# One batch per scan group in a Mamba and mixture-of-experts block: experts beside half of the scan, decay in PSUM

## The chip, the cores and the metric

The kernel runs on one core of a Trainium2 chip, in one launch. The metric is the device time in microseconds. A core has five engines with a queue of instructions each: TensorE (PE in the profile, its weight loads PEld), VectorE (DVE), ScalarE (ACT), GpSimd (POOL) and SyncE (SP, here for DMAs only). They wait for each other by semaphores. The order on each engine is the order in which the program's text issues the instructions; nothing reorders it.

## The reference, cut to what matters

The input x is 4 batches of 128 channels and 256 tokens. The first half of the block is a Mamba layer over four chunks of 32 channels, the second a mixture of 16 experts. All arithmetic is float32.

```python
# first half, for each batch and each of 4 chunks (32 channels -> 64 inner)
xn = layer_norm(x); xi, z = split(xn_chunk @ in_proj)
xc = silu(causal_conv4(xi) + conv_b)
dt_raw, B, C = split(xc @ x_proj)                 # ranks 2, 16, 16
dt = softplus(dt_raw @ dt_proj + dt_b)
for t in range(256):                              # state h: 64 x 16
    h = exp(dt_t * A) * h + (dt_t * xc_t) * B_t
    y_t = sum over the 16 states of h * C_t
y = (y + xc * D) * silu(z); ym = y @ out_proj + skip * xn_chunk
x = x + layer_norm(ym) @ proj + proj_b
# second half, for each token of 128 channels
t = layer_norm(x); logits = t @ router            # 16 experts
w0, w1 = softmax(top 2 of logits)
out = x + sum over e of w_e * ((silu(t @ gate_e) * (t @ up_e)) @ down_e)   # 128 -> 256 -> 128
```

## The kernel before, in words

**Groups and steps.** A tile has 128 partitions and 512 columns. In the scan two chunks of 64 inner channels fill the partitions. A scan group (`gr`) is one pair of chunks for a half of the batches (`hb`, two batches of 256 tokens side by side), so there are four groups; the two groups of half 0 come first. A group has 16 steps, one per state number s; step k = 16 gr + s. In a step:

- PE spreads row s of B over the partitions (`spread_b`), and later row s of C (`spread_c`), each one matmul from 64 rows (`bank<-BC,sel`);
- ACT makes the decay `exp(A_s dt)` in SBUF (`decay`, L447), two steps ahead in a ring of three, and copies B from its PSUM bank to SBUF for POOL (`copy_b`, L441) in the steps whose input POOL makes;
- POOL (`scan_input`, L288) or, for odd steps below 50, DVE (`input_on_dve`, L638) multiplies dt x by B to the input u;
- DVE runs two scans of 256 columns, one per batch (`scan`, L650), and multiplies the states by C (`weigh`, L661);
- PE adds the result into a PSUM bank by an identity matmul (`sum_state`); from step 48 on POOL adds it in SBUF instead (`add_state`, L295).

Behind the last step of a half, a **back chain** of 13 items (`back(hb, i)` on PE, ACT and DVE) does the output projection, two layer norms, the projection, the router, top 2 and the gates, for 512 tokens at once.

**Experts.** A slot is one expert and one half f of its 256 hidden channels, for the 512 tokens of a half: 64 slots. Gate and up products are three passes in a reduced format (high and rest parts of weights and tokens, `product`, L938, L939, L808), each of 512 columns. ACT takes the tanh of the gate (L512), DVE gates (`gate`, L748) and multiplies by the up product (`hidden`, L762); the tokens come scaled by the expert's weight (`scale_tokens` on DVE, L744, `round_scaled` on ACT, L499, `split_scaled` on POOL, L301). `down` adds into one bank, in float32 for the first half, in three reduced passes for the second.

**Stages.** Front (load, norm, projections, convolution, softplus of group 0); steps 0 to 49 alone, with the softplus polynomials of later groups, one of six DVE operations per step, and the back chain of half 0 in steps 33 to 47; then 14 expert slots of half 0 with one step each (`beside`); then the back chain of half 1 in the slots behind them (`back_item`; its PE items 3, 7 and 11 are put behind the next slot's gate product, `LATE`), then the experts of half 1. `keep_warm` issues small matmuls whose result nobody reads; steps 0 to 7 have two each, ahead of `spread_b`.

**Banks.** Before, two PSUM banks for B and two for C, alternating, to step 49; gate and up products have two banks each.

## Time and profile before

| | |
|---|---|
| runs | 388.32, 388.85, 393.81 us; median 388.85 |
| profiled execution | 391.65 us, span 389.8 us |
| PE | 338.6 us busy, 87% |
| DVE | 334.0 us, 86% |
| POOL | 199.6 us, 51% |
| ACT | 196.5 us, 50% |
| mean granted TensorE clock | 0.881 |

The span reaches from the first to the last instruction; 1.85 us of the profiled time lie around it. A line such as `L650 DVE TENSOR_TENSOR_SCAN ring<-ring 128x256` names the source line, engine, operation and tiles (`ring` holds u, the copy of B, the states, the weighed states and the decays; `bank` is PSUM). In a timeline the first number is the start and the second the length, up to the last write; the next instruction of the engine can start a little before that, so a cost in a full queue is taken from start to start. `x2` behind a row is two instructions merged. A float32 matmul stands as two records. What follows in brackets is the idle time of the engine ahead of the row and who ended it. The clock column gives the granted TensorE clock: 1.00 is 2.4 GHz, 0.50 is 1.2 GHz, and a value between them a stretch with both.

### The profile page before, as it was taken

What the parts mean: (1) busy time and instruction counts of PE and PEld (TensorE: products, weight loads), DVE (VectorE), ACT (ScalarE), POOL (GpSimd) and SP (SyncE); (2) the same over time, 40 slices, a digit from 0 to 9 for tenths busy, and PEclk for the clock granted to TensorE, in tenths of its full rate; (3) what the DMA queues carried; (4) which work ended last, traced back from release to release, by engine and by line L of the source; (5) the groups of instructions that cost most, each with busy time, mean ns of one, the idle gap of its engine ahead of it and who ended that gap; (6) DMA issues with size and microseconds to landing.
All of it is one profiled execution on the core that took longest, in us unless ns stands there. A gap on an engine that the chain in (4) does not pass through costs nothing. (4 is left out here: it accounts for less than half of the span.)

```text
span 389.8 us, 3634 instructions
## 1 busy us (share of the span) xinstructions
PE 338.6 (87%) x986; PEld 173.1 (44%) x986; DVE 334.0 (86%) x518; ACT 196.5 (50%) x303; POOL 199.6 (51%) x167
## 2 busy tenths in 40 slices
PE   8793769997979879877878778799998999999996
PEld 5420434432223222232334334345565667777774
DVE  2699999779999999999999999996769686667774
ACT  3974622243434544464745554236783366666661
POOL 4447661224232331321477777745562277888882
PEclk9987565557586999996989998899999999999999
DMA  6592000000000000000000000000000000000000
GB/s 201 168 280 90 2 1 1 0 0 1 0 3 0 0 0 0 1 2 0 0 0 2 0 0 2 0 0 1 2 1 0 1 29 0 1 2 0 0 3 27
DMA packets 6644, 7.95 MB, mean 20 GB/s; under 512 B 352, under 2 KB 5472, under 8 KB 6624
## 3 DMA queue, kind: packets, MB, share of 16 engines
q1 hardware_dynamic: 6480, 7.34, 6.3%
q10 hardware_dynamic: 144, 0.38, 0.3%
q8 instruction: 8, 0.13, 0.2%
q14 instruction: 12, 0.10, 0.1%
HBM read 7.20 MB, written 0.52 MB: 20 GB/s over the span
## 5 line engine op out<-in xcount | busy, mean ns | idle before, releaser
L650 DVE TENSOR_TENSOR_SCAN ring<-ring 128x256 f32<-128x256 f32 x128 | 107.6, 880 | 0.0
L288 POOL TENSOR_TENSOR ring<-dtx,ring 128x512 f32<-128x512 f32 x39 | 56.3, 1445 | 97.0 <-ACT ring L441 63.8
L808 PE MATMUL bank<-BC,sel 64*128 64x512 f32 x128 | 55.7, 592 | 33.9 <-DVE ring L661 23.0
L447 ACT ACTIVATE ring<-dt,cst,A 128x512 f32<-128x512 f32 x64 | 51.3, 809 | 52.7 <-DVE ring L650 52.2
L512 ACT ACTIVATE dt<-bank,cst 128x512 f32<-128x512 f32 x64 | 44.0, 687 | 58.1 <-PE bank L808 58.1
L808 PE MATMUL bank<-ring,ident 128*128 128x512 f32 x96 | 70.0, 818 | 0.3 <-DVE y L670 0.2
L808 PEld LDWEIGHTS bank<-BC,sel 64*128 64x128 f32 x128 | 20.9, 217 | 104.3 <-DVE ring L661 59.5
L748 DVE SCALAR_TENSOR_TENSOR dt<-dt,bank 128x512 f32<-128x512 f32 x64 | 43.8, 684 | 26.5 <-ACT dt L512 26.5
L301 POOL TENSOR_TENSOR xs_lo<-xc,xs_hi 128x512 fp32r<-128x512 f32 x32 | 43.7, 1364 | 28.0 <-ACT xs_hi L499 28.0
L661 DVE TENSOR_TENSOR ring<-ring,bank 128x512 f32<-128x512 f32 x63 | 41.9, 664 | 3.9 <-PE bank L808 3.8
L441 ACT ACTIVATE ring<-bank 128x512 f32<-128x512 f32 x39 | 22.9, 586 | 28.2 <-PE bank L808 28.2
L938 PE MATMUL bank<-tn_hi,Wg_hi 128*128 128x512 f32 x64 | 32.0, 500 | 0.0
L938 PE MATMUL bank<-xs_hi,Wu_hi 128*128 128x512 f32 x64 | 28.0, 437 | 0.0
L295 POOL TENSOR_TENSOR y<-y,ring 128x512 f32<-128x512 f32 x15 | 19.3, 1285 | 14.9 <-DVE ring L661 14.9
L499 ACT ACTIVATE xs_hi<-xc 128x512 fp32r<-128x512 f32 x32 | 20.0, 625 | 13.1 <-DVE xc L744 13.1
L808 PE MATMUL bank<-xs_hi,Wu_lo 128*128 128x512 f32 x64 | 25.9, 404 | 0.0
L939 PE MATMUL bank<-xs_lo,Wu_hi 128*128 128x512 f32 x64 | 25.8, 403 | 0.0
L808 PE MATMUL bank<-tn_hi,Wg_lo 128*128 128x512 f32 x64 | 25.4, 397 | 0.0
L939 PE MATMUL bank<-tn_lo,Wg_hi 128*128 128x512 f32 x64 | 25.4, 397 | 0.0
L808 PEld LDWEIGHTS bank<-ring,ident 128*128 128x128 f32 x96 | 18.1, 236 | 15.9 <-issue 14.2
L333 POOL TENSOR_TENSOR hid_lo<-y,hid_hi 128x512 fp32r<-128x512 f32 x16 | 20.7, 1294 | 8.7 <-ACT hid_hi L506 8.7
L762 DVE TENSOR_TENSOR zs<-dt,bank 128x512 f32<-128x512 f32 x32 | 21.8, 682 | 2.8 <-DVE dt L748 0.4
(134 smaller groups left out, 561.0 us busy)
## 6 DMA issues: line engine op xcount, KB each, us to landing
ring<-gate_w SPq DMA_DIRECT2D x4, 256.0 KB, 5.0
ring<-up_w SPq DMA_DIRECT2D x4, 256.0 KB, 5.3
X<-x SPq DMA_DIRECT2D x2, 256.0 KB, 4.3
sq<-gate_w SPq DMA_DIRECT2D x2, 256.0 KB, 2.7
xm<-gate_w SPq DMA_DIRECT2D x2, 256.0 KB, 3.6
sq<-up_w SPq DMA_DIRECT2D x2, 256.0 KB, 3.5
xm<-up_w SPq DMA_DIRECT2D x2, 256.0 KB, 2.7
out<-X SPq DMA_DIRECT2D x2, 256.0 KB, 2.1
```

The costliest lines, as they stand in the source:

```text
L288: g.tensor_tensor(u[:, k % 3], dtx[:, k // NS, :], Bs[:, copies(k) % 3], ALU.mult)\
L301: g.tensor_tensor(xs_lo[:, k % 2, :], xs, xs_hi[:, k % 2, :].bitcast(F32), ALU.subtract)\
L441: a.activation(Bs[:, copies(k) % 3], bank[b_bank(k)][:], ACT.Copy).then_inc(S["Bs_r"], 1)
L447: a.activation(dA[:, k % 3], dt[:, k // NS, :], ACT.Exp, scale=A[:, s:s + 1], bias=zero)\
L512: a.activation(th[:, f, :], bank[GATE[f]][:], ACT.Tanh, scale=0.5, bias=zero).then_inc(S["th_r"], 1)
L650: v.tensor_tensor_scan(h[:, k % 3, t], dA[:, k % 3, t], u[:, k % 3, t], 0.0, ALU.mult, ALU.add).then_inc(S["scan_r"], 1)
L661: v.tensor_tensor(dst, h[:, k % 3], bank[c_bank(k)][:], ALU.mult).then_inc(S["hc_r"], 1)
L748: v.scalar_tensor_tensor(th[:, f, :], th[:, f, :], 1.0, bank[GATE[f]][:], ALU.add, ALU.mult)\
L762: v.tensor_tensor(hid[k % 2][:, f, :], th[:, f, :], bank[UP[f]][:], ALU.mult).then_inc(S["hid_r"], 1)
L808: return t.matmul(o, w, r, start=start, stop=stop).then_inc(S[name], 1)
L938: t.matmul(bank[b][:], w_hi, hi, start=first, stop=False)
L939: t.matmul(bank[b][:], w_hi, lo, start=False, stop=False)
```

## The change

- **Groups.** A group is one batch with all four chunks: the two pairs lie side by side in the 512 columns. The back chain of batch b needs group b alone and has 256 columns. It runs in turns (`group_turn`): turn o of batch b at step 16 (b+1) + o. Batch 0's runs in steps 16 to 31, those of batches 1 and 2 beside the experts and steps 32 to 63, batch 3's beside items 32 to 47.
- **Experts.** An item is one expert for one batch, both hidden halves side by side: 64 items. Its products are twelve passes of 256 columns. Items 0 to 31 have one step each (steps 32 to 63). While they do, gate and up have one bank each (`gate_bank`, `up_bank`). Down is in reduced passes for the last 16 items only. The tokens of two items are scaled by one DVE operation; the gates' spread reads 128 rows.
- **Scan.** The decay goes to a PSUM bank: two banks in steps 0 to 31, one afterwards (`da_bank`), and `decay` waits for the scan that last read it. The first column of each pair is kept at zero, so one scan of 512 columns serves both pairs. All inputs u are POOL's. C has one bank. States are summed by PE up to step 31, by POOL from 32 on.
- **Norms.** A matmul with `M` (identity less mean) gives centred values straight into PSUM; output projection, skip, norm gain and bias are folded into prepared weights.
- **Softplus.** The logarithm's polynomial is written as two quadratics, each a Square on ACT into PSUM and one DVE operation, where DVE had six; the input's positive part and magnitude come from DVE, the final sum from POOL.
- **Loads.** Each weight chunk has its own staging buffer; eight of sixteen are rounded and split during steps 2 to 23.

The three item loops at the end of the diff are ACT's, DVE's and PE's, in this order.

```diff
-POOL0 = 3 * NS
-LEAD_END = POOL0 + 2
-SCAN_SLOTS = 14
-LATE = (3, 7, 11)
+FIRST = 2 * NS
+ITEMS = BATCH * E
+BESIDE = STEPS - FIRST
+SPLIT0 = 3 * E
...
+        def da_bank(k):
+            return k % 2 if k < FIRST else 0
+        def gate_bank(n):
+            return 1 if n < BESIDE else (1, 0)[n % 2]
+        def up_bank(n):
+            return 5 if n < BESIDE else (5, 2)[n % 2]
...
+        def step_at(slot):
+            return FIRST + slot
+        def group_turn(k, first=1):
+            b, o = divmod(k, NS)
+            return (b - 1, o) if b - 1 in range(BATCH) else (None, None)
...
             def decay(k):
-                if k >= 3:
-                    act.wait_ge(S["scan_r"], 2 * (k - 2))
+                if k % NS == 0:
+                    act.wait_ge(S["dt_r"], k // NS + 1)
+                if before(da_bank, k):
+                    act.wait_ge(S["scan_r"], before(da_bank, k))
                 s = k % NS
-                a.activation(dA[:, k % 3], dt[:, k // NS, :], ACT.Exp, scale=A[:, s:s + 1], bias=zero)\
-                    .then_inc(S["dA_r"], 1)
+                rows = [v.rearrange("p (q t) -> p q t", t=T)[:, :, 1:T] for v in (bank[da_bank(k)][:], dt[:, k // NS, :])]
+                a.activation(rows[0], rows[1], ACT.Exp, scale=A[:, s:s + 1], bias=zero).then_inc(S["dA_r"], 1)
...
+            for n in range(ITEMS):
+                k = step_at(n)
+                gate_tanh(n)
+                if k + 1 < STEPS:
+                    decay(k + 1)
                 if k + 3 < STEPS:
                     copy_b(k + 3)
+                back(*group_turn(k), True)
+                if n % 2 == 0 and n // 2 + 1 < ITEMS // 2:
+                    round_scaled(n // 2 + 1)
...
             def scan(k):
-                for b in range(2):
-                    t = slice(b * T, (b + 1) * T)
-                    v.tensor_tensor_scan(h[:, k % 3, t], dA[:, k % 3, t], u[:, k % 3, t], 0.0,
-                                         ALU.mult, ALU.add).then_inc(S["scan_r"], 1)
+                v.tensor_tensor_scan(h[:, k % 3], bank[da_bank(k)][:], u[:, k % 3], 0.0, ALU.mult, ALU.add)\
+                    .then_inc(S["scan_r"], 1)
...
+            def factor_1(b):
...
+                v.scalar_tensor_tensor(part, bank[R][:], LOG1P_SCALE * QUAD1[1], dt[:, b, :], ALU.add, ALU.mult)\
+                    .then_inc(S["t1_r"], 1)
...
+            for n in range(ITEMS):
+                k = step_at(n)
+                if n % 2 == 0 and n // 2 + 1 < ITEMS // 2:
+                    scale_tokens(n // 2 + 1)
+                gate(n)
+                if k < STEPS:
+                    scan(k)
+                hidden(n)
+                if FIRST < k <= STEPS:
+                    weigh(k - 1)
+                back(*group_turn(k))
...
+            for n in range(ITEMS):
+                k = step_at(n)
+                if n % 2 == 0 and n // 2 + 1 < ITEMS // 2:
+                    spread_gate(n // 2 + 1)
+                gate(n)
+                if FIRST < k <= STEPS:
+                    spread_c(k - 1)
+                if k + 3 < STEPS:
+                    spread_b(k + 3)
+                up(n)
+                for j in downs(n):
+                    down(j)
+                back(*group_turn(k))
```

On ACT beside the experts, before, with the semaphores waited for (L512 tanh, L447 decay, L441 copy of B, L499 rounding of the scaled tokens):

```order
L512 ACTIVATE dt<-bank,cst 128x512 [waits hid_r,g_r]
L447 ACTIVATE ring<-dt,cst,A 128x512 [waits scan_r]
L441 ACTIVATE ring<-bank 128x512 [waits u_r,pB]
L499 ACTIVATE xs_hi<-xc 128x512 [waits up_r,xs_r]
L512 ACTIVATE dt<-bank,cst 128x512 [waits hid_r,g_r]
```

The same place in the change, up to turn 3 of a back chain (L512 tanh, L463 decay, L454 copy of B, L506 rounding, L478 a Square of the back chain):

```order
L506 ACTIVATE xs_hi<-xc 128x512 [waits up_r,xs_r]
L512 ACTIVATE dt<-bank,cst 128x512 [waits hid_r,g_r]
L463 ACTIVATE bank<-dt,cst,A 128x2x255 [waits scan_r]
L454 ACTIVATE ring<-bank 128x512 [waits u_r,pB]
L478 ACTIVATE sq<-bank,cst 128x256 [waits op_r]
L512 ACTIVATE dt<-bank,cst 128x512 [waits hid_r,g_r]
```

The order of the kinds is the same; the decay between two tanh operations is now that of the next step and waits for the scan of this one, and the back chain stands between them while steps still run.

On PE, the variance matmul of the second layer norm in half 1, before (L938, L939 and L808 with `Wg` the gate product, with `Wu` the up product):

```order
L938 MATMUL bank<-tn_hi,Wg_hi 128x512 [waits m_r]
L939 MATMUL bank<-tn_lo,Wg_hi 128x512
L808 MATMUL bank<-tn_hi,Wg_lo 128x512
L808 MATMUL bank<-sq,mean_w 128x512 [waits sq_r]
L938 MATMUL bank<-xs_hi,Wu_hi 128x512 [waits hid_r]
```

The same matmul in the change, turn 7 of batch 1 (L990 the down product of an earlier item, L931 the next gate product):

```order
L990 MATMUL bank<-y,Wd 128x256 [waits hid_r]
L990 MATMUL bank<-y,Wd 128x256
L794 MATMUL bank<-sq,mean_w 128x256 [waits tsq_r]
L794 MATMUL bank<-CE,sel_e 128x256 [waits xs_r,cel_r]
L794 MATMUL bank<-CE,sel_e 128x256
L931 MATMUL bank<-tn_hi,Wg_hi 128x256 [waits m_r]
```

It stood behind the next slot's gate product and now stands ahead of it.

## Rows read from the trace of the kernel before

**Rows 1.** Busy time by stage: start:end, length, then busy us (x instructions) of PE, PEld, DVE, ACT, POOL.
```profile
48.50:84.30 35.80, 32.52 (x63) 14.17 (x63) 30.80 (x46) 9.46 (x14) 12.19 (x9) 0.54 0.00 0
84.30:123.00 38.70, 34.28 (x60) 10.81 (x60) 38.66 (x61) 15.67 (x23) 12.08 (x9) 0.68 0.00 1
123.00:190.20 67.20, 54.56 (x134) 18.77 (x132) 66.78 (x127) 33.22 (x51) 17.84 (x14) 0.95 0.00 0
190.20:256.70 66.50, 52.94 (x149) 26.75 (x148) 65.62 (x81) 31.18 (x48) 49.47 (x35) 0.92 0.00 0
256.70:312.20 55.50, 54.20 (x184) 31.82 (x184) 42.57 (x84) 32.02 (x49) 25.18 (x20) 1.00 0.00 1
312.20:383.50 71.30, 71.30 (x286) 52.03 (x284) 50.49 (x77) 44.11 (x75) 56.17 (x45) 1.00 0.01 5
```

**Rows 2.** Timeline of DVE, one step at the high clock: start, length, engine, line, operation.
```profile
130.04 1.26 DVE L650 TENSOR_TENSOR_SCAN ring<-ring 128x256 f32<-128x256 f32 x2
131.23 0.65 DVE L661 TENSOR_TENSOR ring<-ring,bank 128x512 f32<-128x512 f32 x1
131.81 0.67 DVE L638 TENSOR_TENSOR ring<-dtx,bank 128x512 f32<-128x512 f32 x1
```

**Rows 3.** Timeline of DVE, one slot with a step beside it.
```profile
220.38 0.68 DVE L748 SCALAR_TENSOR_TENSOR dt<-dt,bank 128x512 f32<-128x512 f32 x1
220.98 2.42 DVE L650 TENSOR_TENSOR_SCAN ring<-ring 128x256 f32<-128x256 f32 x2
223.32 0.66 DVE L762 TENSOR_TENSOR zs<-dt,bank 128x512 f32<-128x512 f32 x1
```

**Rows 4.** Timeline of POOL in the same stretch.
```profile
224.66 1.29 POOL L295 TENSOR_TENSOR y<-y,ring 128x512 f32<-128x512 f32 x1 [0.19 <-DVE ring L661]
```

**Rows 5.** Timeline of PE at the low clock, in and after the padded steps.
```profile
73.14 1.22 PE L819 MATMUL bank<-mean_w 128*128 128x128 f32 x4
...
81.62 0.79 PE L808 MATMUL bank<-BC,sel 64*128 64x512 f32 x2
82.34 2.07 PE L808 MATMUL bank<-ring,ident 128*128 128x512 f32 x2
```

**Rows 6.** Timeline of PE at the high clock, the same two steps.
```profile
86.46 0.51 PE L808 MATMUL bank<-BC,sel 64*128 64x512 f32 x2
86.89 1.12 PE L808 MATMUL bank<-ring,ident 128*128 128x512 f32 x2
```

**Rows 7.** Timeline of PE in the expert stage, one slot.
```profile
257.32 0.40 PE L939 MATMUL bank<-tn_lo,Wg_hi 128*128 128x512 f32 x1
257.56 0.40 PE L808 MATMUL bank<-tn_hi,Wg_lo 128*128 128x512 f32 x1
...
258.49 1.02 PE L808 MATMUL bank<-y,Wd 128*128 128x512 f32 x2
```

**Rows 8.** Timeline of DVE ahead of the first scan.
```profile
29.05 5.06 DVE L612 CAST Wu_hi<-ring 128x512 fp32r<-128x512 f32 x4
...
43.92 4.03 DVE L587 TENSOR_TENSOR dtx<-dt 128x512 f32<-128x512 f32 x3
```

**Rows 9.** Timeline of ACT: a slot's three kinds, and a table load.
```profile
223.44 0.81 ACT L447 ACTIVATE ring<-dt,cst,A 128x512 f32<-128x512 f32 x1 [1.40 <-DVE ring L650]
224.16 0.57 ACT L441 ACTIVATE ring<-bank 128x512 f32<-128x512 f32 x1
226.12 0.69 ACT L512 ACTIVATE dt<-bank,cst 128x512 f32<-128x512 f32 x1 [1.39 <-PE bank L808]
...
286.66 1.28 ACT L484 ACT_TABLE_LOAD   x1
```

**Rows 10.** Timeline of DVE, the small arithmetic of the routing.
```profile
294.75 0.36 DVE L718 TENSOR_TENSOR chk<-iota_e,topf 128x64 f32<-128x64 f32 x2
```

**Rows 11.** Timeline of PE, 24 small matmuls ahead of the projections.
```profile
10.58 2.84 PE L819 MATMUL bank<-mean_w 128*128 128x128 f32 x24
```

**Rows 12.** Groups by line and shape: weight loads of an expert, busy, mean ns.
```profile
L938 PEld LDWEIGHTS bank<-tn_hi,Wg_hi 128*128 128x128 f32 x64 | 12.0, 187 | 12.7 <-issue 10.6 <-DVE dt L748 1.3
```

More of the change, by code:

```diff
@@ L315, in _ @@
-            for slot in range(FH * E):
-                k = beside(slot)
-                if k is not None and k + 1 < STEPS:
+            scan_input(0)
+            for k in range(FIRST):
+                scan_input(k + 1)
+                gr, o = soft_turn(k)
+                if o == 3:
+                    add_relu(gr)
+                if o == 4:
+                    scan_source(gr)
+                c = late_chunk(k)
+                if c is not None:
+                    split_rest(c)
+            split_scaled(0)
@@ L614, in _ @@
+            dve.wait_ge(S["rest0"], 2)
+            for b in (0, 1):
+                positive(b)
+                magnitude(b)
             bc_rest(0)
[L615 to L616 removed]
+            for b in (2, 3):
+                positive(b)
+                magnitude(b)
             bc_rest(1)
[L618 to L624 removed]
@@ L766, in _, with result @@
+            def result(b):
+                dve.wait_ge(S["yd_r"], (b + 1) * E)
+                v.tensor_tensor(X[:, b, :], X[:, b, :], bank[sum_bank(b)][:, 0:T], ALU.add).then_inc(S["res_r"], 1)
+            for k in range(FIRST):
                 scan(k)
@@ L855, in _ @@
[L855 to L875 removed]
+            pe.wait_ge(S["mean_c"], 1)
@@ L1011, in _, with product @@
-            for slot in range(FH * HALVES * E - 3, FH * HALVES * E):
-                down(slot // FH, slot % FH)
+                back(*group_turn(k))
+                if k < WARM_STEPS:
+                    keep_warm(2, 6)
+            spread_gate(0)
+            for k in (FIRST - 2, FIRST - 1):
+                sum_state(k)
+            def product(o, w_hi, w_lo, hi, lo, name, first=True, last=True):
+                t.matmul(o, w_hi, hi, start=first, stop=False)
+                t.matmul(o, w_hi, lo, start=False, stop=False)
+                o_ = t.matmul(o, w_lo, hi, start=False, stop=last)
+                if name is not None:
+                    o_.then_inc(S[name], 1)
```

1298 lines of the change are left out of this document (618 added, 680 removed).

## The prediction

> **What bounds the kernel now.** I read the busy time by stage first [rows 1]: ahead of the first scan (to 48.5 us), steps 0 to 49 of the scan alone (48.5 to 190.2), 14 expert slots with a step beside each (190.2 to 256.7), slots 14 to 31 with the second half's back chain (256.7 to 312.2), slots 32 to 63 (312.2 to 383.5), and 6.3 us of end. DVE is busy over 98% of the stretch from 84.3 to 256.7; PE is nearly full from 256.7 on and 100% from 312.2, where a slot takes 71.3 / 31 = 2.3 us.
>
> The timeline of DVE says what that busy time is. Undisturbed, a step's two scans of 256 take 1.19 us start to start and the weighing by C 0.58 [rows 2]. Beside the experts the same pair of scans takes 2.34 us [rows 3]; two of its operands lie in SBUF, and POOL works all the time (49.5 of 66.5 us) [rows 1, 4]. L661 and L762, which read a PSUM bank, keep 0.65 to 0.66 us in both places. So DVE's scans queue behind POOL, and a slot costs 66.5 / 14 = 4.75 us.
>
> PE sets the early steps: its clock is at 0.54 of full, so mostly at the 1.2 GHz level [rows 1]. There a step's B and C spreads take 0.73 us side by side, the identity sum 2.0 and the padding of the first eight steps 1.16 [rows 5]; at the 2.4 GHz level they take 0.43 and about 1.0 [rows 6].
>
> **Part 1, ahead of the first scan: 48.5 to 37 us.** DVE is full there from 24 us on. Gone from it are eight of twelve weight casts (about 8 us; four alone take 5.06), the four squares (three take 4.03) and three of six softplus operations (about 2) [rows 8]: some 14 to 15. Added are eight operations for the positive part and the magnitude, at 0.6 each as L661 in [rows 2]: 5. The centring by DVE goes too (1.3). What is left over of some 11 us is the gain only if ACT keeps up: its chain of sigmoid, three squares, a table load, the first copy and decay becomes the path. I take 11.5 off, between 8 and 14. The weight chunks have a buffer each, so SP's queue waits for nothing; the eight late ones are rounded by ACT and split by POOL during steps 2 to 23, which is in the loads below.
>
> **Part 2, 32 steps alone: 88 us.** DVE needs for a step one scan of 512. No such row exists: at the element rate of [rows 2] (two of 256 in 1.19) it is 1.13, bounded by 1.07 (no fixed cost) and 1.19. With the weighing that is 1.75, plus 0.25 for the softplus. POOL now makes every input u, at 1.25 start to start as in [rows 4], and with sources, sums and eight late weight rests 2.17 a step in steps 0 to 15. PE at the low level needs 0.73 + 2.0 + 1.16 = 3.9 in the eight padded steps and 2.73 after. The low level is what the trace shows over the first 36 us of scanning (0.54), although PE is busy in 32.5 of 35.8 us, so I take 8 x 3.7 + 8 x 2.75 = 52; then 16 steps at 1.75 + 0.5 for batch 0's back chain on DVE (its halved width makes it about 7.5 us) = 36. Bounds: 71 (all at the high level, POOL's 2.17) and 105 (all at the low one, 3.25 for the last 16). The trace has 2.83 us a step now, so 32 of them cost nearly what they did; 18 steps, 51 us, leave this stage. Handing over to the experts costs 2.5 us: spread, scale, round and split of the first pair stand in a row.
>
> **Part 3, 32 items with a step beside each: 172 us.** An item is one expert for 256 tokens, both halves of the hidden width: the work of a slot. Loads per item at the high level, start to start: DVE 0.60 + 1.13 + 0.58 + 0.58 + 0.30 = 3.2; POOL 1.25 x 2.5 = 3.1; PE twelve products of 256 columns at 0.12, two spreads 0.55, down 0.95, gate spread 0.13: 3.1 [rows 3, 4, 6, 7]. The scan now reads its decay from PSUM, so POOL's hold on it should go, as L661 shows.
>
> None of them is the bound. ACT's order is tanh(n), decay(k+1), copy(k+3), rounding of every second item, tanh(n+1), and decay(k+1) has one bank beside the experts, so it waits for scan(k), which DVE starts only after the gate of n. Before, the decay was two steps ahead in a ring of three. The loop: gate 0.60, scan 1.20, decay 0.74, copy 0.52, rounding 0.27, tanh 0.69 = 4.03 us with the latencies between [rows 3, 9]. No row shows ACT writing PSUM: I keep 0.81 long for the decay; at 0.69, the shortest full-width row, the loop is 3.9. 32 x 4.03 = 129.
>
> The back chains of batches 1 and 2 now stand in this loop, for 13 turns each. Two turns hold two table loads and two operations on ACT: 2 x 1.28 + 1.0 = 3.55 each, ahead of the next tanh [rows 9]. In turns 3, 5, 6, 7 and 9 PE's back matmul stands ahead of the next gate product and waits for ACT's or DVE's operation at the item's end: operation 0.4, matmul 0.45, product 0.9, tanh 0.69, less the 0.8 (odd item) or 1.3 that DVE waits for the tanh anyhow: 1.2 to 1.8, together 8.1. Turn 11 has ten small operations on DVE first, 0.18 each [rows 10], in place of the 0.4: 3.0. Turns 1, 10 and 12, mostly inside those waits: 1.8. Sum 20 per batch, 40 in all; I allow 12 to 24. 3 us more for stretches at the low level, as this stage has now (0.92).
>
> **Part 4, the last 32 items: 91.5 us.** PE is the bound again: 16 x (12 x 0.122 + 0.95 + 0.13) + 16 x (18 x 0.122 + 0.13) = 41 + 37 = 78. The halved product's 0.122 is not in the trace; 512 columns take 0.24, and a 256-cycle matmul with its own load takes 2.84 / 24 = 0.118 [rows 7, 11]. Its upper bound is 0.187, the weight load's whole length [rows 12]. Batch 3's back chain adds 9 (now about 55.5 - 18 x 2.5 = 11 for a chain twice as wide [rows 1]), two late downs 2, the end (split, rest, result, output) 4, less 1.5 counted above.
>
> **The sum.** 37 + 88 + 2.5 + 172 + 91.5 = 391 us against a span of 389.8. The profiled run took 391.65, 1.85 around its span, and lies 2.8 over the median 388.85: 391 + 1.85 - 2.8 = **390 us**. By stage, first what is now and then what I expect: to the first scan 48.5 and 37; steps alone 141.7 and 90.5 with the handing over; the first 32 slots 122 and 172; the rest 77.6 and 91.5. The steps that leave the second stage come back in the third.
>
> **Rivals.**
> (A) The forecast, 390, chance 0.42.
> (B) The clock stays at the high level in the steps alone. For it: DVE no longer holds PE up, and from 123 us on the trace has 0.95 [rows 1]. Against: PE was busy for 91% of the first 36 us of scanning and the clock stayed at the 1.2 GHz level for most of it. 16 early steps at 2.17: 52 - 35 = 17 less, 373. Chance 0.20. The Trainium skill, "TensorE: Matmul & The Clock Gate", Part 1, says the opposite rule: throttled is the default and activity releases it. By that rule the sum would be 373; the first stage of rows 1 does not follow it.
> (C) The back turns overlap better than a sum of waits, as ACT and DVE work ahead in the gaps: 10 instead of 20 a batch, 370. Chance 0.14.
> (D) Slower: the clock falls in the shared stage. PE waits there in a quarter of each item, and in the turns with a back matmul the product before the tanh lies in the loop. It decides once the level is low in most of them: 14 turns x 0.7 = 10, and the steps alone at the upper bound add 16: 416. For it: 0.54 and 0.68 in the first two stages. Chance 0.13.
> (E) Slower: weight loads no longer hide behind 256 columns. The point is a product over 0.13. At 0.187: 480 products in the last stage x 0.065 = 31, and 6 in the shared turns: 427. Chance 0.07. The same page, section on the back-to-back issue gap, gives 81 ns for 128 columns and 131 for 512 in a stream with loads; between them, halves would cost 1.5 times the whole. This trace's whole is 240 ns, not 131. By that ratio the estimate would be 0.17 a product and 419 us.
> (F) The change doesn't do what it says: the scan is still held by POOL. In the loop that is 1.2 us x 32: 428. Against: no PSUM row is ever stretched. Chance 0.04.
>
> Two per cent is 8 us, about what a measurement of this kernel can tell from no change. Within A I give 0.34 to 382 to 398, 0.04 to each side. Faster: 0.04 + 0.20 + 0.14 = 0.38; same 0.34; slower 0.28. A's own range is 380 to 401. The range of 8 in 10 takes in B, C and D: 366 to 416.
>
> **What would show it.** L650: 64 scans of 512 at 1.2 us, none near 2. First scan near 37 us. Item distance 4.0 in plain turns, DVE idle before the gate (L743) for ACT's tanh, 0.8 us on average; 6 to 7.5 us between gates in turns 4 and 8. Granted clock of steps 0 to 15 near 0.5; at 1.0, B is right. Products 0.12 apart in the last stage; POOL near 80% in the shared stage. The forecast fails if tanh is not what DVE waits for there.

## The result: 441.6 us, slower by 13%

The changed kernel takes 441.6 us (median of 4 runs, 439.2 to 442.8), beside 390.2 for the kernel before: a ratio of 1.130, 95% interval 1.119 to 1.140. The forecast was 390 and its range ended at 416. The profiled execution took 440.5 us with a span of 438.4. Some executions of a kernel are 1 to 2% slower than its others; ratios here compare the faster ones, and the table below gives no stages for e8, whose profiled execution was a slower one.

The stages of the changed kernel, cut at its first scan, its first gate (L743) and the gates of items 16 and 32 (columns as in [rows 1]):

```profile
37.33:145.88 108.55, 88.01 (x204) 37.04 (x203) 69.15 (x97) 57.47 (x94) 60.16 (x48) 0.75 0.00 1
145.88:239.76 93.88, 64.09 (x316) 51.43 (x316) 60.61 (x96) 43.80 (x69) 45.62 (x37) 0.82 0.00 1
239.76:337.80 98.04, 64.53 (x321) 51.85 (x321) 62.34 (x99) 41.75 (x65) 47.84 (x39) 0.86 0.01 2
337.80:438.40 100.60, 83.15 (x595) 78.51 (x594) 60.19 (x108) 50.76 (x83) 51.68 (x41) 0.95 0.02 5
```

In [rows 1] DVE is over 98% busy for 170 us. Now no engine is full over any of the four stages: PE, the busiest, has 81, 68, 66 and 83%, and is full only behind the gate of item 48. Where every engine waits in turn, the time is the length of a ring through several of them, and busy shares no longer tell it. Beside the forecast, in us:

| | forecast | measured |
|---|---|---|
| to the first scan | 37 | 37.3 |
| 32 steps alone, to the first gate | 90.5 | 108.5 |
| items 0 to 31 | 172 | 191.9 |
| the rest | 91.5 | 100.6 |

Four of the costliest groups of the profile of after (busy, mean ns, then the idle time before them and what ended it) say what was bought:

```profile
L463 ACT ACTIVATE bank<-dt,cst,A 128x510 f32<-128x510 f32 x64 | 49.9, 779 | 96.1 <-DVE ring L652 96.1
L743 DVE SCALAR_TENSOR_TENSOR dt<-dt,bank 128x512 f32<-128x512 f32 x64 | 43.9, 686 | 80.1 <-ACT dt L512 80.1
L652 DVE TENSOR_TENSOR_SCAN ring<-bank,ring 128x512 f32<-128x512 f32 x64 | 77.8, 1216 | 15.3 <-POOL ring L304 7.3
L512 ACT ACTIVATE dt<-bank,cst 128x512 f32<-128x512 f32 x64 | 43.8, 684 | 82.5 <-PE bank L933 82.4
```

All 64 scans take 1.21 to 1.22 us, where a pair took 2.34 beside the experts [rows 3]: POOL's hold on them is gone. What took its place is in the last column: DVE's gate waits for ACT's tanh, the tanh for PE's gate product, ACT's decay for DVE's scan.

**One item with a back turn.** The timeline of after from the gate of item 5 to that of item 6. TensorE's turn 5 of batch 1's back chain stands at the end of item 5, ahead of the gate product of item 6:

```profile
174.08 0.69 DVE L743 SCALAR_TENSOR_TENSOR dt<-dt,bank 128x512 f32<-128x512 f32 x1 [5.04 <-ACT dt L512]
174.68 1.22 DVE L652 TENSOR_TENSOR_SCAN ring<-bank,ring 128x512 f32<-128x512 f32 x1
...
176.99 0.42 DVE L684 TENSOR_TENSOR chk<-bank,sq 128x256 f32<-128x256 f32 x1
...
177.46 1.22 PE L794 MATMUL bank<-chk,proj_w 128*128 128x256 f32 x2 [5.95 <-DVE chk L684]
...
178.12 0.99 PE L794 MATMUL bank<-CE,sel_e 128*128 128x256 f32 x2
...
178.91 0.41 PE L931 MATMUL bank<-tn_hi,Wg_hi 128*128 128x256 f32 x1
...
179.97 0.41 PE L933 MATMUL bank<-tn_hi,Wg_lo 128*128 128x256 f32 x1
...
180.43 0.69 ACT L512 ACTIVATE dt<-bank,cst 128x512 f32<-128x512 f32 x1 [3.20 <-PE bank L933]
...
181.15 0.69 DVE L743 SCALAR_TENSOR_TENSOR dt<-dt,bank 128x512 f32<-128x512 f32 x1 [1.31 <-ACT dt L512]
```

Follow it down: the bank for the next gate product was free from 174.8 on, but its queue has the back matmul first, and that waits for DVE's last operation of the item (L684). PE stands still for 5.95 us; then back matmul, spread of the routing weights and gate product run one after the other, at the 1.2 GHz level (products 0.21 apart), and only then the tanh. Gate to gate is 7.07 us where a plain item (one without a turn) takes 3.5 to 4.3.

### The profile page after: what moved, and what is told of

Its sections match the earlier page's. It is cut to its first block and busy times, and to the rows that moved or that the text cites. A ratio compares the mean times of both kernels' runs of the same rounds, so it can differ in the third digit from the quotient of the medians.

```text
span 438.4 us, 4893 instructions
## 1 busy us (share of the span) xinstructions
PE 329.9 (75%) x1576; PEld 238.7 (54%) x1576; DVE 278.8 (64%) x443; ACT 221.4 (51%) x352; POOL 223.8 (51%) x199
## 5 line engine op out<-in xcount | busy, mean ns | idle before, releaser
L463 ACT ACTIVATE bank<-dt,cst,A 128x510 f32<-128x510 f32 x64 | 49.9, 779 | 96.1 <-DVE ring L652 96.1
L743 DVE SCALAR_TENSOR_TENSOR dt<-dt,bank 128x512 f32<-128x512 f32 x64 | 43.9, 686 | 80.1 <-ACT dt L512 80.1
L304 POOL TENSOR_TENSOR ring<-dtx,ring 128x512 f32<-128x512 f32 x64 | 81.9, 1290 | 12.6 <-ACT ring L454 12.6
L652 DVE TENSOR_TENSOR_SCAN ring<-bank,ring 128x512 f32<-128x512 f32 x64 | 77.8, 1216 | 15.3 <-POOL ring L304 7.3
L512 ACT ACTIVATE dt<-bank,cst 128x512 f32<-128x512 f32 x64 | 43.8, 684 | 82.5 <-PE bank L933 82.4
L454 ACT ACTIVATE ring<-bank 128x512 f32<-128x512 f32 x64 | 37.3, 583 | 16.0 <-PE bank L794 15.5
L663 DVE TENSOR_TENSOR ring<-ring,bank 128x512 f32<-128x512 f32 x62 | 41.6, 671 | 4.2 <-PE bank L794 4.2
L931 PE MATMUL bank<-tn_hi,Wg_hi 128*128 128x256 f32 x128 | 43.7, 341 | 0.2 <-DVE dt L743 0.2
L931 PE MATMUL bank<-xs_hi,Wu_hi 128*128 128x256 f32 x128 | 42.0, 328 | 0.0
L932 PE MATMUL bank<-tn_lo,Wg_hi 128*128 128x256 f32 x128 | 38.9, 304 | 0.0
L933 PE MATMUL bank<-tn_hi,Wg_lo 128*128 128x256 f32 x128 | 38.7, 302 | 0.0
L932 PE MATMUL bank<-xs_lo,Wu_hi 128*128 128x256 f32 x128 | 38.0, 297 | 0.0
L933 PE MATMUL bank<-xs_hi,Wu_lo 128*128 128x256 f32 x128 | 38.0, 297 | 0.0
L990 PE MATMUL bank<-zs,Wd 128*128 128x256 f32 x96 | 28.4, 424 | 7.8 <-DVE X L759 7.8
L931 PEld LDWEIGHTS bank<-xs_hi,Wu_hi 128*128 128x128 f32 x128 | 26.4, 206 | 9.4 <-issue 8.9
L931 PEld LDWEIGHTS bank<-tn_hi,Wg_hi 128*128 128x128 f32 x128 | 27.4, 214 | 1.1 <-DVE dt L743 0.4
```

The lines of the kernel that those rows point to most:

```text
L304: g.tensor_tensor(u[:, k % 3], dtx[:, k // NS, :], Bs[:, k % 3], ALU.mult).then_inc(S["u_r"], 1)
L463: a.activation(rows[0], rows[1], ACT.Exp, scale=A[:, s:s + 1], bias=zero).then_inc(S["dA_r"], 1)
L512: a.activation(th[n % 2], bank[gate_bank(n)][:], ACT.Tanh, scale=0.5, bias=zero).then_inc(S["th_r"], 1)
L652: v.tensor_tensor_scan(h[:, k % 3], bank[da_bank(k)][:], u[:, k % 3], 0.0, ALU.mult, ALU.add)\
L663: v.tensor_tensor(dst, h[:, k % 3], bank[c_bank][:], ALU.mult).then_inc(S["hc_r"], 1)
L743: v.scalar_tensor_tensor(th[n % 2], th[n % 2], 1.0, bank[gate_bank(n)][:], ALU.add, ALU.mult)\
```

## The experiments

All kernels but the combined ones are the changed kernel with one edit. The table has for each the median, the ratio to the kernel before with its 95% interval, and from its profile, in us: first scan to first gate ("alone"), the 16 items of batch 1's back chain, the 16 of batch 2's, and gate 32 to gate 63. e3, e12 and e14 leave part of the work out and only price it.

| | median | ratio | alone | items 0-15 | 16-31 | 32-63 |
|---|---|---|---|---|---|---|
| changed kernel | 441.6 | 1.130 (1.119-1.140) | 108.5 | 93.9 | 98.0 | 93.5 |
| e1 PE's turns late | 413.9 | 1.057 (1.049-1.066) | 108.6 | 82.7 | 86.4 | 90.4 |
| e2 scan first | 416.4 | 1.065 (1.056-1.073) | 106.5 | 79.7 | 86.2 | 95.8 |
| e3 no table loads | 421.4 | 1.077 (1.067-1.088) | 105.8 | 87.6 | 91.8 | 89.3 |
| e4 two C banks | 436.2 | 1.115 (1.106-1.124) | 97.8 | 93.6 | 97.6 | 96.5 |
| e5 combined | 385.3 | 0.987 (0.979-0.994) | 99.8 | 75.9 | 77.3 | 86.2 |
| e6 result early | 439.6 | 1.123 (1.113-1.133) | 108.4 | 93.8 | 96.0 | 95.4 |
| e7 padding | 441.7 | 1.130 (1.120-1.139) | 106.1 | 92.1 | 98.7 | 95.2 |
| e8 combined, padded | 388.8 | 0.998 (0.991-1.004) | | | | |
| e9 softplus spread | 440.5 | 1.126 (1.114-1.138) | 107.3 | 94.3 | 97.8 | 96.6 |
| e10 weights early | 432.3 | 1.107 (1.095-1.118) | 106.1 | 91.6 | 97.1 | 94.4 |
| e11 combined 2 | 378.8 | 0.972 (0.964-0.980) | 94.1 | 72.6 | 74.1 | 89.3 |
| e12 combined, no loads | 365.7 | 0.939 (0.929-0.949) | 98.8 | 68.8 | 71.0 | 80.9 |
| e13 split later | 434.5 | 1.125 (1.114-1.135) | 100.5 | 93.6 | 97.7 | 94.9 |
| e14 half state sum | 440.3 | 1.138 (1.125-1.151) | 105.3 | 93.5 | 98.0 | 96.4 |
| e15 steps alone, all | 416.0 | 1.074 (1.065-1.083) | 81.3 | 92.3 | 98.0 | 96.1 |
| e16 combined 3 | 364.7 | 0.943 (0.936-0.949) | 82.0 | 72.6 | 74.6 | 89.4 |

Each experiment ran beside the kernel before, on four chips in all; its median was 391.6 to 392.5 us on each, its single runs 385.3 to 395.4. So small differences are read from the stages of the profiles, and there each stage has its own spread. Kernels that don't differ in the stage have 105.8 to 108.6 us for the steps alone, 92.3 to 94.3 for items 0 to 15 and 93.5 to 96.6 for the last. A difference inside these is read from nowhere.

### The shared stage

**e1: TensorE's back turns behind the next gate product.**

```diff
 gate(n)
+if n:
+    back(*group_turn(k - 1))
...
 for j in downs(n):
     down(j)
-back(*group_turn(k))
```

> The changed kernel takes 441.6 us. Here TensorE's part of a back turn stands behind the gate product of the next item instead of ahead of it; nothing else moves. Theory (a back turn is dear because the gate product, and with it the tanh and the gate, queue behind a matmul that waits for DVE's or ACT's last operation of the item): turns 3, 5, 6, 7, 9 and 11 lose 1.5 to 3 us each, 10 to 15 a batch; batches 1 and 2 give all of it back and batch 3 half: 405 to 418 us. Rival (the turns are dear because ACT's and DVE's own back operations and the low clock stand in the loop, and the wait only moves to the up product): 432 us or more.

28 us less. The odd turns with a back matmul fall to the length of plain items: in batch 1 the turns 3, 5, 7, 9 from 6.7, 7.1, 6.8, 7.1 to 4.1, 3.8, 4.1, 4.4 us, turn 11 from 9.4 to 6.7. Turns 4 and 8 keep their 8.0. Turns 6 and 10 become longer (5.6 and 5.3 to 6.5), since PE's queue now meets them a product later. The timeline of e1 for the item above:

```profile
172.49 0.38 PE L931 MATMUL bank<-tn_hi,Wg_hi 128*128 128x256 f32 x1 [3.08 <-DVE dt L743]
...
174.67 0.42 DVE L684 TENSOR_TENSOR chk<-bank,sq 128x256 f32<-128x256 f32 x1
174.80 0.68 ACT L512 ACTIVATE dt<-bank,cst 128x512 f32<-128x512 f32 x1
...
175.14 1.22 PE L794 MATMUL bank<-chk,proj_w 128*128 128x256 f32 x2 [1.67 <-DVE chk L684]
```

The tanh runs at 174.80, beside DVE's L684; PE's back matmul waits as before, but nobody waits for PE.

**e2: the scan ahead of the gate.**

```diff
+if k < STEPS:
+    scan(k)
 gate(n)
-if k < STEPS:
-    scan(k)
 hidden(n)
```

> DVE starts the scan of an item ahead of the gate instead of behind it, in the 32 items that hold a step; nothing else moves. Theory (a plain item is 4.0 us long because gate, scan, decay, copy, rounding and tanh stand in one ring): the decay into PSUM no longer waits for the gate, plain items fall from 4.0 to 3.3 or 3.4, and the dear ones by the same: 32 x 0.65 = 21 us, 415 to 428 us. Rival (the scan only pushes the gate back by 1.2 us, and with it the next gate product, which waits for the single gate bank): no change or slower, 438 to 455 us.

25 us less, 0.8 an item where 0.65 was expected. Breaking the ring of the forecast shortens the items as it should. A plain item in the timeline of e2:

```profile
224.37 1.22 DVE L652 TENSOR_TENSOR_SCAN ring<-bank,ring 128x512 f32<-128x512 f32 x1
...
225.51 0.66 DVE L743 SCALAR_TENSOR_TENSOR dt<-dt,bank 128x512 f32<-128x512 f32 x1
225.62 0.78 ACT L463 ACTIVATE bank<-dt,cst,A 128x510 f32<-128x510 f32 x1 [1.13 <-DVE ring L652]
...
227.34 0.68 ACT L512 ACTIVATE dt<-bank,cst 128x512 f32<-128x512 f32 x1
227.46 1.22 DVE L652 TENSOR_TENSOR_SCAN ring<-bank,ring 128x512 f32<-128x512 f32 x1
```

Decay and gate run side by side, and the next scan starts beside the tanh: 3.09 us from scan to scan, where the changed kernel takes 3.5 to 4.3 for a plain item. An item then costs about what DVE works in one (3.2 us by the forecast's rows).

**e3: no table loads.**

```diff
-if tables:
-    a.preload_act_table_set("natural_log_exp_and_others")
...
-a.activation(sq[:, b, :], ..., ACT.Ln, bias=eps)
+a.activation(sq[:, b, :], ..., ACT.Copy)
...
-if tables:
-    a.preload_act_table_set("exp_and_others")
```

> The four table loads of a back chain beside the experts are left out (3 batches, 12 loads of 1.28 us), with ACT's Ln replaced by a copy of the same size, so that only the loads go; the normalisation of these batches is therefore not computed. Theory (the loads stand ahead of the next tanh, as the forecast had it): turns 4 and 8 fall from 8.0 to about 5.5 us, 2.56 x 2 x 2 = 10 us in the shared stage and up to 5 in batch 3: 426 to 432 us. Rival (what the next tanh waits for in these turns is TensorE, not ACT): 438 us or more.

20 us less, more than expected. Turns 4 and 8 fall from 8.0 to 5.1 in the shared stage and from 5.4 to 2.4 in batch 3: 2.9 to 3.0 for two loads of 1.28, or 18 us for all twelve. The other 2 are inside what the steps alone vary by. So the loads stand whole in the ring, in the last stage too, where the forecast had counted them among 9 us for everything. In the combined kernel e12 shows the same price:

> The combined kernel without the twelve table loads beside the experts, Ln replaced by a copy, so that the normalisation of three batches is not computed. In the changed kernel the loads cost 20 us, 1.7 for each load of 1.28. Theory (each load stands whole in the ring of its item, in the combined kernel too): 12 x 1.28 = 15 us less, 368 to 372 us. Rival (with the scan ahead of the gate and TensorE's turns behind the product, ACT has slack that hides them): 378 us or more.

19.6 us for twelve loads, 1.6 each by the medians; the turns fall from 6.3 to 3.4, 1.45 a load. The freed order hides none of it.

**e6: the result of a batch early.** DVE's `result(b)` moves from the end of item 16b + 18 to behind its gate.

> The result of a batch (DVE's addition that frees the bank of the expert sums) stands behind the gate of its item instead of at the item's end. Theory (the down product of the first expert of the next batch waits for it, and the next item's gate product queues behind that down): item 18 falls from 10.0 to about 6.5 us and item 34 from 5.8 to 7.4 to about 4, so 6 us in all: 434 to 437 us. Rival (another wait ends these items): 439 us or more.

```diff
 gate(n)
 if k < STEPS:
     scan(k)
+if n % E == LAG and n >= E:
+    result(n // E - 1)
 hidden(n)
```

The stretch of item 18, 10.0 us in the changed kernel (9.0 to 10.3 where this order is the same), is 7.8 in e6, and items 16 to 31 take 2 us less; item 34 (5.8 to 7.5 over the kernels) shows nothing certain, and 2 us of the median is within what the runs vary. The wait is real (PE's down product stood 4.84 us for L759), its price by itself is about 2 us and not 6: turn 2's three back matmuls stand behind it in the same queue. e1, which moves those, has 7.5 for item 18; both edits together (e5, below) have 4.6.

**e7 and e8: padding for the clock.** Three unused matmuls an item:

```diff
 for j in downs(n):
     down(j)
+if n < BESIDE:
+    pe.wait_ge(S["xs_r"], n // 2 + 2)
+    keep_warm(WARM_ITEM, SPREAD)
```

> Three padding matmuls of 128x128 (about 0.2 us each at the high clock) stand at the end of each of the 32 items with a step, ahead of the back turn; their results are used by nothing. Theory (a third of the cost of the dear turns is that TensorE's clock falls to 1.2 GHz in its waits, so the gate product takes 1.3 instead of 0.7 us): the granted clock of the shared stage rises from 0.84 to 0.93 or more and the time falls by 5 to 15: 427 to 436 us. Rival (the padding does not hold the clock, or costs in the ring what it gives back): clock under 0.88, or 439 to 455 us.

The same stretch in the changed kernel and in e7:

```profile
145.00:290.00 145.00, 97.07 (x473) 77.43 (x471) 90.18 (x137) 65.59 (x103) 70.02 (x57) 0.84 0.01 2
```

```profile
145.00:290.00 145.00, 108.58 (x627) 91.77 (x626) 90.63 (x137) 65.56 (x104) 71.61 (x58) 0.89 0.01 2
```

The granted clock rises from 0.84 to 0.89, between the theory's 0.93 and the rival's 0.88, and the time stays. e8 is 3 to 4 us above e5, within its rival.

> The combined kernel with the same three padding matmuls in each of the 32 items, here behind the up product. Theory: as for the padding alone, 3 to 10 us below the combined kernel. Rival: 0 to 10 us above it, as the ring is shorter there and TensorE's own load is nearer to it.

This doesn't show that the low clock is free, because the padding missed the turns that are dearest. In e7's turn 5 PE still stands for 5 us behind the padding, and its gate product is again 0.21 a pass (six passes, the first and the last shown):

```profile
176.16 1.22 PE L795 MATMUL bank<-chk,proj_w 128*128 128x256 f32 x2 [5.28 <-DVE chk L685]
...
177.61 0.41 PE L932 MATMUL bank<-tn_hi,Wg_hi 128*128 128x256 f32 x1
...
178.68 0.41 PE L934 MATMUL bank<-tn_hi,Wg_lo 128*128 128x256 f32 x1
```

Turns 5 and 9 are 7.1 us in both kernels. In turns 3 and 7 of batch 1, where e7's products are 0.12 apart for 0.21, the turns fall from 6.7 and 6.8 to 6.0. In batch 2 those two turns run at 0.12 in the changed kernel too and take 5.9 and 6.0. Of the kernels with this order, turn 5 came at 0.12 in one only, in batch 2 of e3 (where turn 4 before it has no loads), and took 5.8 for 7.1. So the low level costs 0.7 us in a turn 3 or 7 and, by that one case, 1.3 in a turn 5 or 9. That is some 7 us of the stage's 192 for turns 3, 5, 7 and 9, an estimate (2 x 0.7 + 4 x 1.3). The larger part of a turn's cost is the wait.

**e10: the routing weights spread early.** 

```diff
+    if k == FIRST - 2:
+        spread_gate(0)
-spread_gate(0)
...
-if n % 2 == 0 and n // 2 + 1 < ITEMS // 2:
-    spread_gate(n // 2 + 1)
 gate(n)
...
 up(n)
+if n % 2 and n // 2 + 2 < ITEMS // 2:
+    spread_gate(n // 2 + 2)
```

> TensorE spreads the routing weights of a pair of experts ahead of the down product of the item before, and those of the first pair ahead of the last two state sums; nothing else moves. Theory (at the handover, 11.9 us between the last scan alone and the first beside an expert, and in every second item DVE's scaling of the tokens waits for a spread that stands behind a state sum or a back matmul): 3.5 us at the handover and 0.5 to 1 us in each of some twelve dear items: 427 to 434 us. Rival (the scaling waits in the shadow of the tanh, only the handover gains): 437 to 439 us.

9 us less by the medians, 5 by the spans (438.4 to 433.0). Turns 5, 9 and 11 fall by 0.5 each. The handover, from the last scan alone to the first beside an expert, falls from 11.9 to 10.1 us, but it is 10.8 in e3 and e7 without this edit, so 0.7 to 1.8 us of that is the edit's.

### The steps alone

The distances between scans in the changed kernel are 1.7 us in eight steps and 3.8 or more in 13 of 31, which hold 60 of the 97 us from the first scan to the last before the experts. Two kinds of dear step stand in its timeline (DVE, ACT and POOL):

```profile
60.76 1.21 DVE L652 TENSOR_TENSOR_SCAN ring<-bank,ring 128x512 f32<-128x512 f32 x1
...
62.00 0.78 ACT L463 ACTIVATE bank<-dt,cst,A 128x510 f32<-128x510 f32 x1 [1.89 <-DVE ring L652]
62.72 0.58 ACT L454 ACTIVATE ring<-bank 128x512 f32<-128x512 f32 x1
63.20 0.68 ACT L419 ACTIVATE bank<-dtx,cst 128x512 f32<-128x512 f32 x1
63.81 0.62 ACT L368 ACTIVATE Wu_hi<-stage_buf 128x512 fp32r<-128x512 f32 x1
63.91 0.69 DVE L624 SCALAR_TENSOR_TENSOR dt<-bank,sq 128x512 f32<-128x512 f32 x1 [1.37 <-ACT bank L419]
64.50 1.26 POOL L280 TENSOR_TENSOR Wu_lo<-stage_buf,Wu_hi 128x512 fp32r<-128x512 f32 x1 [5.16 <-ACT Wu_hi L368]
64.52 1.21 DVE L652 TENSOR_TENSOR_SCAN ring<-bank,ring 128x512 f32<-128x512 f32 x1
```

DVE's softplus factor (L624) waits for ACT's quadratic, which waits behind decay and copy for the scan just made: a ring of 3.8 us. And POOL stands 5.16 us in its queue for the rounding of a late weight chunk (L368), with the next input u behind it. The waits of the changed kernel from 40 to 126 us, total, times and longest:

```profile
POOL Wu_lo L280 <- ACT Wu_hi L368: 27.3, 8, 6.8
ACT bank L463 <- DVE ring L652: 26.1, 19, 4.3
PEld bank L794 <- DVE ring L663: 22.1, 13, 3.8
```

The third is the single C bank: PE's next spread of C stands until DVE has weighed by the last one (L663). **e4** gives C a second bank and takes it from B:

```diff
 def b_bank(k):
-    return (2, 7)[k % 2] if k < LAST_B2 else 2
+    return 2
-c_bank = 3
+def c_bank(k):
+    return (3, 7)[k % 2] if k < LAST_C2 else 3
```

> In the 32 steps alone the spreads of C get two PSUM banks and the spreads of B one (before: B two, C one). Theory (TensorE waits there for DVE's weighing to free the one C bank, and idles in it): the steps alone fall from 108.6 to 95 to 100 us, the kernel to 428 to 434. Rival (TensorE's own work at the low clock, 2.7 us a step, and ACT's and POOL's order set the steps): under 4 us, 438 us or more.

**e9** spreads the softplus over seven steps, on ACT, DVE and POOL (`soft_at(k, d)` names the batch whose turn d is in step k):

```diff
-if o == 1: quadratic_1(gr)
-if o == 2: quadratic_2(gr)
+for d, f in ((0, square_z), (1, quadratic_1), (3, quadratic_2)):
...
-if o == 1: factor_1(gr)
-if o == 2: factor_2(gr)
+for d, f in ((2, factor_1), (4, factor_2)):
...
+for d, f in ((5, add_relu), (6, scan_source)):
```

> In the steps alone the softplus of batches 1 to 3 is spread over seven steps instead of five: DVE's two factors come one step behind ACT's quadratics instead of in the same step, and POOL's sum and source behind them. Theory (in six steps of the changed kernel scan, decay, copy, quadratic and factor stand in one ring of 3.8 us, where a free step takes 1.7): these steps fall to about 2.2, 6 x 1.6 = 10 us less in the steps alone: 430 to 434 us. Rival (TensorE's own work at the low clock and the single C bank end these steps anyhow): 438 us or more.

**e13** moves POOL's split of a late chunk by two steps:

```diff
-c = late_chunk(k)
+c = late_chunk(k - 2)
 if c is not None:
     split_rest(c)
```

> POOL takes the rest of a late weight chunk two steps after ACT's rounding instead of in the same step. Theory (POOL stands in the rounding's wait, which itself stands behind the decay and so behind the scan, with the next but one u queued behind it; the eight steps after a late chunk are 4.5 to 5 us long in the changed kernel): these steps fall to about 3, 8 to 12 us less in the steps alone: 430 to 434 us. Rival (TensorE at the low clock, 2.7 us a step and 3.9 with padding, or the single C bank ends these steps anyhow): 437 us or more.

**e14** halves TensorE's state sum and leaves half of it out:

```diff
-mm(bank[STATE_SUM[b]][:], ident[:], hc[:, k % 3], ...)
+w = N if s == 0 else N // 2
+mm(bank[STATE_SUM[b]][:, 0:w], ident[:], hc[:, k % 3, 0:w], ...)
```

> TensorE's identity sum of the states of batches 0 and 1 covers 256 of 512 columns (the other half is left out, so the output is not the reference's): a step alone costs TensorE 1.0 us less at the low clock. Theory (TensorE at 1.2 GHz is what sets the steps from 16 on, one C bank or not): 8 to 15 us less in the steps alone, 427 to 434 us. Rival (the waits in a ring through POOL, ACT and DVE set them): 437 us or more.

**e15** joins e4, e9, e13 and the early first spread:

> All four edits of the steps alone together and nothing in the shared stage: two banks for C, the early first spread, the spread softplus, the later split of the weight rests. Each alone left the others' waits in place (two C banks gave 5 us, the spread softplus 1). Theory (the steps alone are several rings side by side, each as long as the next, and only together do they give way): the steps alone fall from 108.5 to 88 to 92 us, about the 90.5 of the forecast, the kernel to 421 to 425. Rival (the low clock stays and keeps them over 98): 430 us or more.

In the stage itself e4 gives 10.7 us and e13 8.0. e10 has 2.4 and e9 1.2 less than the changed kernel, both inside the spread of kernels that don't differ there. By the median e4 gives 5.4; in its profile the first scan is 1.9 us later and the last stage 3.0 longer, as in other kernels that don't differ there. e9 was wrong as a single cause: its 3.8 steps fell to 1.7 and 2.5, and the steps of the late chunks beside them grew to 5. Together the four give 27.2, and the stage is 81.3 us long, shorter than the 90.5 of the forecast; e15 ran on one chip with e14, 24 us below it. A piece is worth more once others are gone: in the combined kernels below, the spread softplus (with a move on ACT beside the experts) takes 5.7 us off this stage, and the later split 12.1 more. Rings of like length hide one another.

**The clock in the steps alone.** The stretches 60 to 80 and 80 to 100 us in the changed kernel, in e14 and in e15:

```profile
60.00:80.00 20.00, 14.05 (x28) 4.94 (x27) 12.99 (x16) 11.36 (x19) 12.34 (x10) 0.78 0.00 0
80.00:100.00 20.00, 16.44 (x22) 5.11 (x21) 13.87 (x16) 8.42 (x13) 12.88 (x10) 0.50 0.00 0
```

```profile
60.00:80.00 20.00, 17.28 (x31) 8.01 (x30) 12.70 (x16) 12.16 (x20) 12.50 (x11) 0.50 0.00 1
80.00:100.00 20.00, 14.08 (x24) 5.79 (x23) 14.71 (x16) 8.35 (x13) 12.87 (x10) 0.50 0.00 0
```

```profile
60.00:80.00 20.00, 14.93 (x40) 4.65 (x38) 18.62 (x24) 15.21 (x25) 19.89 (x17) 1.00 0.00 0
80.00:100.00 20.00, 17.26 (x54) 7.12 (x54) 18.16 (x31) 15.30 (x27) 16.76 (x14) 1.00 0.00 0
```

e14's median is that of the changed kernel (440.3 for 441.6). From 80 to 100 us both are at the 1.2 GHz level, e14 with half of each state sum; the steps there are 4.1, 2.5, 7.1 and 1.7 us long in the one and 4.1, 2.5, 6.3 and 1.7 in the other. So PE's work doesn't set most of these steps, the waits do. In e15 the steps follow each other faster, and PE is at 2.4 GHz throughout. The Trainium skill, "TensorE: Matmul & The Clock Gate", Part 1, has activity releasing the clock; these stretches agree as far as the high one holds the most matmul records (40 and 54, against 22 to 31), while by busy time they would not (75% at 1.00 beside 86% at 0.50).

The low level isn't free here either. The changed kernel and e3 have the same order up to the experts, but e3 was at 2.4 GHz where the last state sum of batch 0 ends. The sum and the scan behind it, in the changed kernel and in e3:

```profile
91.40 2.07 PE L794 MATMUL bank<-ring,ident 128*128 128x512 f32 x2
...
95.66 1.21 DVE L652 TENSOR_TENSOR_SCAN ring<-bank,ring 128x512 f32<-128x512 f32 x1
```

```profile
89.75 1.13 PE L790 MATMUL bank<-ring,ident 128*128 128x512 f32 x2
...
92.34 1.21 DVE L648 TENSOR_TENSOR_SCAN ring<-bank,ring 128x512 f32<-128x512 f32 x1
```

The scan before starts at 88.55 and at 87.46, so the step takes 7.1 us at the low level and 4.9 at the high one. DVE waits there for PE's sum (L672), and 0.7 of the 2.2 us is its next operation, L675, which at the low level falls beside POOL's u (1.44 us for 0.72). The changed kernel, e1, e2, e6 and e7 have 7.1 at 0.50, e3 and e10 4.9 at 1.00. e14, with the halved sum at 0.50, has 6.3, and its handover 8.9 for 11.9. PE holds this step and a part of the handover, and the waits hold the others. How much of e15's 27.2 us is the clock that rose with the shorter steps, no run separates: at the low level PE alone needs 2.7 us a step by [rows 5], and half of e15's 31 steps are 1.7 or less.

### The combined kernels

e5 has e1, e2, e4, e6 and e10 in one; e11 adds e9 and moves ACT's Ln and Exp of turns 4 and 8 with the first table load behind the tanh, ahead of the decay; e16 adds e13.

```diff
 gate_tanh(n)
+b, o = group_turn(k)
+if o in (4, 8):
+    rstd(b, o)
 if k + 1 < STEPS:
     decay(k + 1)
```

> All of it at once: TensorE's back turns behind the next gate product, the scan ahead of the gate, two banks for C, the result of a batch right behind the gate of its item, the spread of the routing weights for a pair ahead of the down product of the item before, and the first such spread ahead of the last two state sums. Theory (independent rings and queues, whose gains of 28, 25 and 5 us add up but for what two of them share, plus 6 for the result and 6 for the spreads): 371 to 385 us, which is faster than both kernels. Rival (the back turns are one resource that both large edits free, so the gains overlap by half): 390 to 400 us.

> The combined kernel (385.3 us) with the spread softplus, and with ACT's logarithm and exponential of turns 4 and 8 (and the first of their two table loads) ahead of the decay, right behind the tanh, where ACT waits for the scan. Theory: 8 us less in the steps alone and 1 us less in each of six turns: 369 to 375 us, faster than both kernels. Rival (the steps alone are held by TensorE's low clock, and the decay comes late behind the logarithm): 381 to 388 us.

> The second combined kernel (378.8 us) with the later split of the weight rests. Theory: its steps alone fall from 94 to 88 us or less, 371 to 374 us. Rival (POOL's work only moves, to where the second back chain's steps need it): 377 to 382 us.

e5's five edits bring 69.7 us by their single medians and 56.3 together, at the upper edge of its range. e11 missed its 375 by 4 us and e16 beat its 371 by 6: the late chunks were what still held e11's steps, as for e9. e16 is the fastest, 364.7 us, 5.7% under the kernel before (5.1 to 6.4); each of its runs (up to 366.6) is below every run of that one. Its last stage is 3 us longer than e5's (89.4 for 86.2), as is e11's; no run tells why. Its stages, cut as above:

```profile
36.81:118.83 82.02, 70.10 (x214) 31.32 (x214) 69.84 (x99) 56.35 (x94) 60.28 (x48) 0.88 0.00 1
118.83:191.43 72.60, 58.51 (x321) 45.12 (x321) 62.10 (x98) 43.49 (x69) 46.59 (x38) 0.93 0.00 1
191.43:266.02 74.59, 58.45 (x315) 44.86 (x315) 62.78 (x98) 41.43 (x66) 47.67 (x38) 0.91 0.01 3
266.02:362.50 96.48, 84.07 (x593) 79.58 (x592) 59.74 (x107) 50.75 (x83) 51.31 (x41) 0.95 0.02 5
```

The engines' work is that of the changed kernel (DVE 62.1 us against 60.6 in items 0 to 15, POOL 46.6 against 45.6) in 72.6 us instead of 93.9: nothing but order and banks has changed. The clock rose with it, from 0.82 to 0.93.

## Why the prediction was wrong

**Part 1** held: 37.3 us for 37, and 36.6 to 39.4 over all the kernels.

**Part 2 failed at its method: the waits between engines stood in it at nothing.** It priced a step by the busiest engine at a clock level ("8 x 3.7 + 8 x 2.75", then 1.75 + 0.5) and looked for no ring. Missing were three waits that queues and banks impose, each of which can be read off the program: POOL behind ACT's rounding (8.0 by e13), the C bank (10.7 by e4), the factor behind the quadratic (1.2 by itself in e9, within the spread, and part of the 27.2 in e15). That the first 16 steps came near their price (48.8 us for 52) was luck: they were priced at a clock of 0.5 and ran at 0.78, held by waits. The next 16 had no such offset: from scan 16 to the first gate 59.8 us for 38.5. The bounds 71 to 105 hold the 81.3 of e15, but in e15 the clock is 0.91, so what is sound there is the price per engine at the high level, not the sum of 88. The handover was put at 2.5 us; from the last scan alone to the first beside an expert it is 11.9, since the spread of the weights stands behind a state sum at the low clock, and round, split and a table load behind that. e15 has 8.4 there, e16 6.0.

**Part 3: the ring was right, the turns were not.** Plain items are 3.5 to 4.3 us apart: the four of batch 1 have a mean of 4.04, those of batch 2 3.77 (4.03 forecast). DVE waits for the tanh before the gate, and e2 broke the ring as it should. The step that failed is "20 per batch", with 12 to 24 allowed. Over 16 x 4.03 = 64.5 us the chains cost 29.4 and 33.5. The turns 4 and 8 cost 4.0 each for 3.55 (e3). Turns 3, 5, 6, 7 and 9 were put at 8.1 together and cost 13.1 in batch 1 and 11.5 in batch 2. The formula took an operation, the matmul, the product and the tanh at the high clock, less the wait that DVE had anyhow; it left out the spread of the routing weights in the same queue (e10: 0.5 a turn), and that PE, idle for 6 us, starts at the 1.2 GHz level. For the low level the sum had 3 us over the stage, where the turns alone make some 7, an estimate from e7 and e3. Turn 11 costs 5.4 for 3.0. Item 18 costs 6.0 by itself; that the addition of the result and the down product meet turn 2 there was not foreseen (2 us by e6, 5.4 with e1's order and the rest of e5). Of the 23 us by which the chains pass 40, turns 3, 5, 6, 7 and 9 make 8.4, turn 11 4.8 and item 18 6.0. That these turns cost what they do by their position in PE's queue, e1 shows: it changes nothing else and takes 23 us off this stage.

The remedy needed no chip: the kernel before has its turns 3, 7 and 11 late (`LATE`), and the change drops that. The forecast saw the turns ahead of the product and put a price on them, but did not ask what else stands in that queue and at what clock it starts.

**Part 4** was 9 us short, at the term "adds 9". From gate 32 to gate 48 the chain of batch 3 adds 61.0 - 41 = 20 us; kernels that don't differ there have up to 64.0, so 20 to 23. About 6 of it is table loads by the turns of e3; e1's order has 57.9, 3 to 6 less. After it the items take 2.17 us each, where 2.3 was forecast, with PE busy throughout.

**The rivals.** B, the clock high in the steps alone: no (0.75); but e15 shows its mechanism, and 81 us with it. C, better overlap of the turns: no, the other way. D, the clock: it did fall (0.82 and 0.86), and its price of 0.7 us a turn is what turns 3 and 7 show; but its 10 us is a fifth of the miss and its 416 far off, since the waits that hold PE also cost by themselves. E, weight loads exposed at 256 columns: no, products in the last stage are 0.113 to 0.12 us apart. The Trainium skill, "TensorE: Matmul & The Clock Gate", "Back-to-back issue gap", led to an estimate of 0.17 and 419; half of 1.5 x 0.24 is 0.18, which makes 424. The measurement decides against either. F, scans still held by POOL: no, 1.216 us in the mean. None of the rivals was several rings that hold in turn, and that is what happened. The range ended at 416 because every slow case within it had been built from one engine's clock.

The signs set ahead: scan 1.2, first scan 37, plain items near 4.0 with the tanh as the wait and products 0.12 apart all came true. DVE's idle time before the four plain gates of batch 1 (13 to 16) was 0.6 us in the mean for 0.8. The granted clock of steps 0 to 15 was 0.78, neither 0.5 nor 1.0. Turns 4 and 8 were 8.0, beyond 6 to 7.5, and POOL has 49% instead of 80%, since items were 6 us long in the mean.

## What to carry to other kernels

Once a change frees the engine that was full, add up rings, not loads: for every queue write down what stands ahead of the instruction that starts the next item, and what that waits for. A side chain that is spread one turn per item belongs behind the operation that feeds the next item, on every engine, and table loads in a ring cost at least their length. A low granted clock can come from waits and still lengthen the operations behind them: before padding is called useless, look whether it raised the clock where the ring runs. When several rings have nearly the same length, removing one can show little; try them together before calling a cause innocent.
